# Attention over feature pairs on one core: sixteen identity matmuls first, one transposition later, three loads on another queue

## The chip, the core and the metric

The kernel runs on one core of a Trainium2 chip. Its engines are TensorE (PE, with its weight loads PEld), VectorE (DVE), ScalarE (ACT), GpSimd (POOL) and SyncE (SP), each with its own list of instructions, tied together by semaphores. The metric is device time in microseconds; the number given is a median of runs.

## The reference

512 samples have 33 embedding rows of 128 numbers each, gathered from tables. All 528 pairs of rows are multiplied element by element, go through a 128 x 128 layer with relu, and are scored against the sample's GNN feature. A softmax over the pairs weighs the products, and a three-layer MLP follows. All is fp32.

```python
inner = x[:, row] * x[:, col]                       # 528 pairs
fm = relu(einsum('bpd,ad->bpa', inner, attn_W) + attn_b)
attn = softmax(einsum('ba,bpa->bp', gnn_feature, fm), axis=1)
attn_output = einsum('bp,bpd->bd', attn, inner) * 100.0
h = concatenate([gnn_feature, attn_output, gnn_feature], axis=1)
h = maximum(h @ W_top1 + b_top1, 0.0)
h = maximum(h @ W_top2 + b_top2, 0.0)
y = h @ W_top3
```

## The kernel before

The batch is cut into 4 tiles of 128 samples, and a tile into 32 steps of 4 samples. One step is: VectorE multiplies the pairs of four samples (`product`, L757) into one of two slots of `inner`; TensorE runs six rounds of 352 columns through the attention weights (`pair_products`, L466) into four banks of `x_ps`; ScalarE applies the relu to each round (L700) into `fm`; TensorE takes the scores (`scores`, L478), with a column of GNN features that VectorE has placed (`column`, L773). TensorE's order is: products of step s, then scores of step s - 1. VectorE's `column` of a step waits for the scores two steps back, and the next `product` stands behind it.

The rows come in groups of 128 (4 samples x 32 fields), one group for a step. GpSimd gathers a group with one indirect DMA (L364). For the first tile it issues twelve groups at once (`FIRST_RUN`), then three more after each step's scores (`scores_done`). Four groups are a chunk. Gathered rows have to be turned: TensorE transposes them into `m_ps` (L485 for whole groups, L523 for half rows, two chunks at a time), and VectorE copies them into `e_t` (`copy_chunk`, `copy_half`). Which chunk is turned after which step of the first tile stands in `FIRST_TURNS`, and the copies in `FIRST_COPIES`. The opening is apart: `turn_opening` turns the last field's rows and group 0, `turn_opening_rest` groups 1 to 3, so that the first product can begin early.

Before the steps, TensorE computes the GNN part of the first MLP layer (`gnn_layer(c)`, L587, four chunks of two calls), once `gnn_t` and two parts of `w1` have landed. ScalarE reads each result out (L726). Then it issues three DMAs from its own queue: the third part of `w1`, `w2` and `w3` (L728 to L730), needed in the MLP at the end of the kernel. SyncE starts with four loads, and then waits for `zeros_cleared`, which GpSimd gives in the first tile at step `AHEAD_AT` = 24. The identity `ident` is made by GpSimd at the start (L356, L358).

Of the kernel before, what the change touches and what calls it, by code (L numbers as in the profile page):

```python
# [36 lines left out]
P = 128  # L37
# [54 lines left out]
NEXT_AT = 8  # L92
AHEAD_AT = 24
FOLD_AT = POOL_AT - 2
FIRST_TURNS = {3: (2, 3), 6: (4, 5), 9: (6, 7)}
FIRST_COPIES = {2: 1, 5: 2, 6: 3, 8: 4, 9: 5, 11: 6, 12: 7}
OPENING = 2
LAST_FIELDS_AT = 18
HALF_ROWS = P // 2
# [2 lines left out]
H1, H2 = 512, 256  # L102
# [3 lines left out]
def flat(tensor_ap, offset, dims):  # L106

    return bass.AP(tensor=tensor_ap.tensor, offset=offset, ap=dims)


def build(nc, gnn_cols, gnn_pairs, ids, table, w_top1, b_top1, w_top2, b_top2, w_top3, attn_w_cols, attn_b, out):
    band_dram = nc.dram_tensor("band_scratch", (P, BAND), F32, kind="Internal").ap()

    with ExitStack() as ctx:
# [18 lines left out]
        ident = sb("ident", [P, P])  # L133
# [11 lines left out]
        w1 = sb("w1", [P, K1, H1])  # L145
        w2 = sb("w2", [P, C1, H2])
        w3 = sb("w3", [P, C2])
# [10 lines left out]
        x_ps = ctx.enter_context(nc.psum_tensor("x_ps", [P, 4, BANKF], F32))  # L158
# [11 lines left out]
        w1_attn_loaded = sem("w1_attn_loaded")  # L170
        w23_loaded = sem("w23_loaded")
        ident_zero = sem("ident_zero")
        ident_ready = sem("ident_ready")
# [128 lines left out]
        @block.sync  # L302
        def _(sp):
            sp.dma_start(idx_in[:, :], ids).then_inc(ids_loaded, 16)
            sp.dma_start(gnn_t[:, :], gnn_cols).then_inc(gnn_t_loaded, 16)
            sp.dma_start(attn_w_t[:, :], attn_w_cols).then_inc(attn_w_loaded, 16)
            sp.dma_start(gnn_z[:, :, :], gnn_pairs).then_inc(gnn_z_loaded, 16)

            def store_bands(stage, m0, m1):
                issue_bands(sp, stage, m0, m1)  # L310
                sp.wait_ge(band_stored, bands_per_stage * (stage + 1))

            def load_band(slot, free_at, row, groups=GPB):

                if free_at is not None:
                    sp.wait_ge(pool_done, free_at)
                for r in range(GROUP):
                    sp.dma_start(band[r * SIDE:(r + 1) * SIDE, slot, 0:groups, r, :],
                                 flat(band_dram, row * BAND + r * BAND,
                                      [[WIDE, SIDE], [GROUP * BAND, groups], [1, WIDE]])  # L320
                                 ).then_inc(pool_loaded[slot], 16)

            def load_bands(t):
                for k in range(2):
                    load_band(k, POOL_N * t if t else None, ROWS * k)
                with sp.Fori(1, POOLS // 2) as i:
                    for slot in range(2):
                        load_band(slot, 2 * i + (POOL_N * t + slot - 1), 2 * ROWS * i + ROWS * slot)
                load_band(0, POOL_N * t + POOLS - 1, POOLS * ROWS, LEFT_GROUPS)
                for slot in range(2):  # L330
                    sp.wait_ge(pool_loaded[slot], pool_per_tile[slot] * (t + 1))

            sp.wait_ge(zeros_cleared, 1)
            sp.dma_start(band_dram, zeros[:, :]).then_inc(bands_zeroed, 16)
            sp.wait_ge(bands_zeroed, 16)
            sp.wait_ge(bands_cleared, 2)
            for t in range(LAST):
                store_bands(t, 0, STEPS)
                load_bands(t)

            store_bands(LAST, STAGE_M[0], STAGE_M[1])
            for k in range(L_BATCHES):
                load_band(k % 2, POOL_N * LAST + max(k - 1, 0), ROWS * k)
            issue_bands(sp, LAST + 1, STAGE_M[1], STAGE_M[2])
            issue_tail_bands(sp, 1)

            issue_bands(sp, LAST + 2, STAGE_M[2], STAGE_M[3], turned_around=(0, 1))
            issue_tail_bands(sp, 2)
            sp.wait_ge(y_ready, len(MLP_PARTS))
            sp.dma_start(out.rearrange("b o -> o b"), y[:, :]).then_inc(y_stored, 16)  # L350
            sp.wait_ge(y_stored, 16)
# [103 lines left out]
        def _(pe):  # L455
# [31 lines left out]
            def turn_opening():  # L487

                pe.wait_ge(ident_ready, 1)
                pe.wait_ge(last_gathered[0], 16)  # L490
                pe.transpose(m_ps[:, 1, 0:P], last_rows[:, 0, :], ident[:, :])
                pe.wait_ge(first_gathered, 16)
                turn_group(0, 0, 0).then_inc(turned, 1)
# [16 lines left out]
            def turn_chunks(t, chunks):  # L510

                pe.wait_ge(turn_copied, turns_through(t, chunks[0]) - 1)
                for c in chunks:
                    pe.wait_ge(gathered[t % BUFFERS][c], 16 * CHUNK * (t // BUFFERS + 1)
                               - (16 if t == BUFFERS and c == 0 else 0))
                    for g in range(CHUNK * c, CHUNK * c + CHUNK):
                        if len(chunks) == 1:
                            mm = turn_group(c % 2, t, g)
                        else:
                            at = (g - CHUNK * chunks[0]) * HALF_ROWS  # L520
                            for h in range(2):
                                lo, hi = HALF_ROWS * h, HALF_ROWS * (h + 1)
                                mm = pe.transpose(m_ps[:, h, at:at + HALF_ROWS], rows[lo:hi, t % BUFFERS, g, :],  # L523
                                                  ident[lo:hi, lo:hi])
                mm.then_inc(turned, len(chunks))
# [59 lines left out]
            def gnn_layer(c):  # L585
                for k in (0, 2):
                    mm = pe.matmul(x_ps[:, c, :], w1[:, k, c * P:(c + 1) * P], gnn_t[:, :],  # L587
                                   start=(k == 0), stop=(k == 2))
                mm.then_inc(gnn_layer_done, 1)


            pe.wait_ge(gnn_t_loaded, 16)
            pe.wait_ge(w1_loaded, 32)
            gnn_layer(0)
            turn_opening()
            gnn_layer(1)
            gnn_layer(2)
            turn_opening_rest()
            gnn_layer(3)
# [2 lines left out]
            for t in range(TILES):  # L602
                base = STEPS * t

                pair_products(base, 0, first=t == 0)
                if t == 0:
                    turn_chunks(0, (1,))
                else:
                    scores(base - 1, 1, stop=True)
                pair_products(base + 1, 1)  # L610
                if t > 0:
                    pe.wait_ge(exp_done, t)
                scores(base, 0, start=True)
                for s in range(2, POOL_AT + POOLS if t > 0 else POOL_AT + 2):
                    pair_products(base + s, s % 2)
                    scores(base + s - 1, (s - 1) % 2)
                    if t == 0 and s in FIRST_TURNS:
                        turn_chunks(0, FIRST_TURNS[s])
                    if t > 0 and s >= POOL_AT:
                        pool_step(t - 1, s - POOL_AT)  # L620
                if t == 0:
                    with pe.Fori(1, POOLS // 2) as i:
                        for j in range(2):
                            pair_products(2 * i + (base + POOL_AT + j), j)
                            scores(2 * i + (base + POOL_AT + j - 1), 1 - j)
                if t == LAST:
                    break

                for s in range(POOL_AT + POOLS, STEPS):
                    pair_products(base + s, s % 2)  # L630
                    scores(base + s - 1, (s - 1) % 2)
                    if t > 0 and s == POOL_AT + POOLS:
                        pool_step(t - 1, POOLS)
                    if t == 0 and s == LAST_FIELDS_AT:
                        turn_last_fields()
                    if s == TURN_AT and t > 0:
                        pe.wait_ge(pool_read, POOL_N * t)
                    if s in TURNS:
                        turn_chunks(t + 1, TURNS[s])
# [16 lines left out]
            for g in range(TAIL_GROUPS):  # L656
                k = g // GPB
# [25 lines left out]
        def _(act):  # L683
            def w1_part(k):
                return flat(w_top1, k * P * H1, [[H1, P], [1, H1]])
# [38 lines left out]
            for c in range(C1):  # L724
                act.wait_ge(gnn_layer_done, c + 1)
                act.activation(h1_gnn[:, c, :], x_ps[:, c, :], ACT.Identity,  # L726
                               bias=b1[:, c:c + 1]).then_inc(gnn_layer_read, 1)
            act.dma_start(w1[:, 1, :], w1_part(1)).then_inc(w1_attn_loaded, 16)  # L728
            act.dma_start(w2[:, :, :], w_top2.rearrange("(k p) n -> p k n", p=P)).then_inc(w23_loaded, 16)
            act.dma_start(w3[:, :], w_top3.rearrange("(k p) o -> p (k o)", p=P),  # L730
                          allow_slow_non_contiguous=True).then_inc(w23_loaded, 16)
            for t in range(TILES):
                base = STEPS * t
                relus(base, 0, first=t == 0)
# [262 lines left out]
```

## Time and profile before

| what | value |
|---|---|
| runs before | median 651.45 us (651.18 to 651.52, 3 runs) |
| profiled execution, its own time | 656.16 us |
| its span | 654.4 us |
| TensorE busy | 641.9 us (98%) |
| VectorE, ScalarE, GpSimd busy | 403.6, 417.4, 268.8 us |
| granted TensorE clock, mean | 0.999 |

The span goes from the first to the last instruction of the profile. Busy times of the engines lie beside one another, and a matmul's end is modelled, so TensorE's share is not a share of its peak. Times in rows below are microseconds from the start of the span unless they are marked ns.

### The profile page before, as it was taken

The page shows a single profiled execution, that of the slowest core. Times are in us where ns is not written, and L with a number is a line of the kernel's source. Part 1 is how long each engine was busy: PE and PEld are TensorE (multiplying, and loading weights), DVE is VectorE, ACT ScalarE, POOL GpSimd, SP SyncE. Part 2 cuts the span into 40 slices and gives each one's busy share as a digit, 9 for nine tenths or more (in the row PEclk, how much of TensorE's full clock was granted, in tenths as well). Part 3 has the DMA queues.
Part 4 walks back from the last instruction along what each step waited for, and adds up shares of the span by engine and source line. Part 5 has one row for each costly group of instructions (what it writes and reads, how often), then busy time and mean ns, then how long its engine had stood idle before and what let it go on. Part 6 is the DMA issues. An engine that isn't in the chain of part 4 may idle for free.

```text
span 654.4 us, 22667 instructions
## 1 busy us (share of the span) xinstructions
PE 641.9 (98%) x9596; PEld 328.1 (50%) x9596; DVE 403.6 (62%) x426; ACT 417.4 (64%) x797; POOL 268.8 (41%) x208
## 2 busy tenths in 40 slices
PE   6998999999999999999999999999999999999998
PEld 2444444444444555544444555544444555544566
DVE  3564655656664677676655577766655567764763
ACT  2665666666777566676777556667677666677651
POOL 6787876685656422244746522244101011100010
PEclk9999999999999999999999999999999999999999
DMA  3211111011091111000092111000026011030010
GB/s 117 83 37 37 30 36 30 25 30 64 18 31 27 28 32 26 16 13 18 14 32 30 24 32 30 16 18 6 1 14 15 7 17 18 7 21 8 16 25 8
DMA packets 51286, 17.29 MB, mean 26 GB/s; under 512 B 47553, under 2 KB 48321, under 8 KB 51202
## 3 DMA queue, kind: packets, MB, share of 16 engines
q1 hardware_dynamic: 44738, 6.03, 11.3%
q0 software_dynamic: 4288, 8.66, 5.5%
q8 instruction: 73, 1.20, 0.8%
q10 hardware_dynamic: 2176, 1.32, 0.7%
q14 instruction: 11, 0.09, 0.1%
HBM read 14.10 MB, written 1.89 MB: 24 GB/s over the span
## 4 chain that ended last, share of the span: by engine, by line
PE 91%; DVE 2%; POOL 2%; DMA 2%; another core or an unknown queue 1%; issue 1%; ACT 0%; DVEq 0%; ACTq 0%
PE x_ps L466 66%; PE s_ps L478 16%; PE m_ps L531 4%; POOL rows L364 2%; DVE inner L757 2%; PE m_ps L523 1%; DMA rows<-in_table,idx 1%; PE s_ps L571 1%; PE x_ps L571 1%; PE x_ps L531 1%; DMA idx_in<-in_ids 0%; PE x_ps L560 0%; DVE e_t L809 0%; PE m_ps L560 0%
## 5 line engine op out<-in xcount | busy, mean ns | idle before, releaser
L700 ACT ACTIVATE fm<-x_ps,ab 128x352 f32<-128x352 f32 x768 | 406.0, 555 | 204.3 <-PE x_ps L466 184.2
L466 PE MATMUL x_ps<-inner,attn_w_t 128*32 128x352 f32 x6144 | 480.8, 459 | 2.2 <-issue 0.9
L466 PEld LDWEIGHTS x_ps<-inner,attn_w_t 128*32 128x32 f32 x6144 | 201.5, 110 | 229.7 <-issue 149.4
L757 DVE TENSOR_TENSOR inner<-e_t 128x2112 f32<-128x2112 f32 (+1 forms) x128 | 302.0, 2359 | 19.3 <-PE x_ps L466 16.6
L364 POOL DMA_INDIRECT rows<-in_table,idx x128 | 213.0, 1664 | 196.5 <-PE s_ps L478 179.9
L478 PE MATMUL s_ps<-fm,gnn_col 128*32 128x256 f32 (+1 forms) x2048 | 138.0, 386 | 0.0
L773 DVE COPY gnn_col<-gnn_z 128x8 f32<-128x8 f32 (+1 forms) x120 | 23.9, 199 | 180.0 <-PE s_ps L478 173.0
L478 PEld LDWEIGHTS s_ps<-fm,gnn_col 128*32 128x32 f32 x2048 | 68.7, 110 | 62.4 <-issue 20.5
L392 POOL TENSOR_TENSOR band<-band 128x192 f32<-128x192 f32 (+1 forms) x39 | 26.3, 676 | 145.6 <-DMA band<-band_scratch 145.1
L531 PE MATMUL m_ps<-band,rows 128*32 128x132 f32 x912 | 33.5, 275 | 0.0
L531 PEld LDWEIGHTS m_ps<-band,rows 128*32 128x32 f32 x912 | 27.9, 109 | 7.1
L826 DVE TENSOR_REDUCE attn_out<-pooled 128x396 f32 (+2 forms) x44 | 24.4, 553 | 4.8
L809 DVE COPY e_t<-m_ps 128x512 f32<-128x512 f32 x30 | 19.6, 686 | 8.1 <-PE m_ps L523 6.2
L822 DVE TENSOR_TENSOR pooled<-m_ps,e_t 128x396 f32<-128x396 f32 (+1 forms) x40 | 22.2, 555 | 0.7
L382 POOL COPY e_t<-e_t 128x256 f32<-128x256 f32 x24 | 13.3, 583 | 9.3 <-DVE e_t L809 9.2
L587 PE MATMUL x_ps<-gnn_t,w 128*128 128x512 f32 x16 | 10.3, 790 | 5.4 <-DMA w<-in_W_top 5.4
L523 PEld LDWEIGHTS m_ps<-ident,rows 64*128 64x128 f32 x240 | 8.8, 138 | 7.7 <-issue 6.6
L523 PE MATMUL m_ps<-ident,rows 64*128 64x64 f32 x240 | 11.1, 229 | 0.8 <-DMA rows<-in_table,idx 0.8
L370 POOL DMA_INDIRECT last_rows<-in_table,idx x4 | 7.5, 1871 | 3.8 <-DVE idx L868 2.9
L587 PEld LDWEIGHTS x_ps<-gnn_t,w 128*128 128x128 f32 x16 | 3.8, 260 | 8.9 <-DMA gnn_t<-in_gnn_cols 5.4
L779 DVE COPY gnn_col<-gnn_z 128x4 f32<-128x4 f32 x6 | 1.0, 172 | 11.7 <-PE s_ps L478 11.7
L392 POOL TENSOR_TENSOR tail_band<-tail_band 128x640 f32<-128x640 f32 (+1 forms) x2 | 2.0, 996 | 15.0 <-DMA tail_band<-band_scratch 15.0
(57 smaller groups left out, 86.5 us busy)
## 6 DMA issues: line engine op xcount, KB each, us to landing
band<-band_scratch SPq DMA_DIRECT2D x144, 18.4 KB
rows<-in_table,idx POOLq DMA_INDIRECT x128, 2.5
band_scratch<-zeros SPq DMA_DIRECT2D x1, 784.0 KB, 3.3
w<-in_W_top ACTq DMA_DIRECT2D x3, 256.0 KB
band_scratch<-attn SPq DMA_DIRECT2D x12, 64.0 KB
gnn_z<-in_gnn_pairs SPq DMA_DIRECT2D x1, 512.0 KB
w<-in_W_top ACTq DMA_DIRECT2D x1, 512.0 KB
gnn_t<-in_gnn_cols SPq DMA_DIRECT2D x1, 256.0 KB, 3.8
```

Source lines behind the costliest of these rows:

```text
L364: pool.indirect_dma_start(rows[:, t % BUFFERS, g, :], None, table, bass.IndirectOffsetOnAxis(ap=idx[:, STEPS * t + g:STEPS * t + g + 1], a ...
L392: pool.tensor_tensor(view[:, :, 0:HOPS], view[:, :, 0:HOPS], view[:, :, FIELDS:WIDE], ALU.add).then_inc(done, 1)
L466: mm = pe.matmul(strip(x_ps[:, (ROUNDS * slot + r) % 4, 0:ROUND], c), strip_of(attn_w_t, c), round_of(inner, slot, r), start=True, stop=True)
L478: mm = pe.matmul(s_ps[32 * q:32 * q + 32, h, score_at[h]:score_at[h] + hi - lo], gnn_col[:, slot, q, :], fm[:, slot, q, lo:hi], start=star ...
L523: mm = pe.transpose(m_ps[:, h, at:at + HALF_ROWS], rows[lo:hi, t % BUFFERS, g, :], ident[lo:hi, lo:hi])
L531: mm = pe.matmul(strip(out, c).rearrange("p (r w) -> p r w", w=FIELDS), strip_of(fields, c), bands[:, :, 0:FIELDS], start=True, stop=True)
L700: act.activation(round_of(fm, slot, r), x_ps[:, (ROUNDS * slot + r) % 4, 0:ROUND], ACT.Relu, bias=ab[:, 0:1]).then_inc(fm_ready, 1)
L757: dve.tensor_tensor(inner[:, slot, :, :].rearrange("p q (i k) -> p q i k", k=HOPS), flat(e, at, [[P * WIDE, P], [WIDE, QUADS], [1, FIELDS] ...
L773: dve.tensor_copy(col_at(slot, m - 2, 2), gnn_at(t, m, 0, 2)).then_inc(col_ready, 1)
L809: done = dve.tensor_copy(flat(e_t[t % 2][:, :, :], at, dims + [[1, SIDE]]), src)
L822: dve.tensor_tensor(sums, bank[:, 0:n_rows * FIELDS].rearrange("p (r w) -> p r w", w=FIELDS), flat(e_t[t % 2][:, :, :], row * WIDE, [[P * ...
L826: dve.tensor_reduce(flat(attn_out[:, :], t * P + row, [[BATCH, P], [1, n_rows]]), sums, AX.X, ALU.add).then_inc(pool_summed, 1)
```

## The change

Sixteen fp32 matmuls of the identity with itself stand ahead of TensorE's wait for `gnn_t`; they write 128 columns of `x_ps`, which `gnn_layer(0)` overwrites. The opening turn moves from behind `gnn_layer(0)` to behind `gnn_layer(1)`. The turn of chunk 1 moves from behind the products of step 0 to behind the products of step 1 and the scores of step 0, and its copy from behind step 2 to behind step 3. The three MLP loads leave ScalarE's queue for SyncE's, where they wait for the twelfth `scores_done`.

```diff
-FIRST_TURNS = {3: (2, 3), 6: (4, 5), 9: (6, 7)}
-FIRST_COPIES = {2: 1, 5: 2, 6: 3, 8: 4, 9: 5, 11: 6, 12: 7}
+FIRST_TURNS = {1: (1,), 3: (2, 3), 6: (4, 5), 9: (6, 7)}
+FIRST_COPIES = {3: 1, 5: 2, 6: 3, 8: 4, 9: 5, 11: 6, 12: 7}
+WARM_UPS = 16
+WEIGHTS_AT = 12
...
+            sp.wait_ge(scores_done, WEIGHTS_AT)
+            sp.dma_start(w1[:, 1, :], flat(w_top1, P * H1, [[H1, P], [1, H1]])).then_inc(w1_attn_loaded, 16)
+            sp.dma_start(w2[:, :, :], w_top2.rearrange("(k p) n -> p k n", p=P)).then_inc(w23_loaded, 16)
+            sp.dma_start(w3[:, :], w_top3.rearrange("(k p) o -> p (k o)", p=P),
+                         allow_slow_non_contiguous=True).then_inc(w23_loaded, 16)
             sp.wait_ge(zeros_cleared, 1)
...
+            pe.wait_ge(ident_ready, 1)
+            for _ in range(WARM_UPS):
+                pe.matmul(x_ps[:, 0, 0:P], ident[:, :], ident[:, :], start=True, stop=True)
             pe.wait_ge(gnn_t_loaded, 16)
             pe.wait_ge(w1_loaded, 32)
             gnn_layer(0)
+            gnn_layer(1)
             turn_opening()
-            gnn_layer(1)
             gnn_layer(2)
...
                 pair_products(base, 0, first=t == 0)
-                if t == 0:
-                    turn_chunks(0, (1,))
-                else:
+                if t > 0:
                     scores(base - 1, 1, stop=True)
                 pair_products(base + 1, 1)
                 if t > 0:
                     pe.wait_ge(exp_done, t)
                 scores(base, 0, start=True)
+                if t == 0:
+                    turn_chunks(0, FIRST_TURNS[1])
...
-            act.dma_start(w1[:, 1, :], w1_part(1)).then_inc(w1_attn_loaded, 16)
-            act.dma_start(w2[:, :, :], w_top2.rearrange("(k p) n -> p k n", p=P)).then_inc(w23_loaded, 16)
-            act.dma_start(w3[:, :], w_top3.rearrange("(k p) o -> p (k o)", p=P),
-                          allow_slow_non_contiguous=True).then_inc(w23_loaded, 16)
```

## Rows read from the trace of the kernel before

**Rows 1.** The page, part 4: the chain that ended last, by engine

```profile
PE 91%; DVE 2%; POOL 2%; DMA 2%; another core or an unknown queue 1%; issue 1%; ACT 0%; DVEq 0%; ACTq 0%
```

**Rows 2.** The chain in order of time, 0 to 60 us: start, length, what

```profile
16.34 4.46 DMA rows<-in_table,idx
...
32.27 3.59 DMA rows<-in_table,idx
...
52.90 6.87 another core or an unknown queue
```

**Rows 3.** Timeline, TensorE and its loads: start, length, engine, line, tiles, count, [idle before]

```profile
5.40 3.75 PE L587 MATMUL x_ps<-gnn_t,w 128*128 128x512 f32 x4 [5.40 <-DMA w<-in_W_top]
...
9.16 0.42 PE L485 MATMUL m_ps<-ident,rows 128*128 128x128 f32 x1
...
11.08 0.34 PEld L587 LDWEIGHTS x_ps<-gnn_t,w 128*128 128x128 f32 x1 [0.52 <-issue]
11.72 0.19 PEld L587 LDWEIGHTS x_ps<-gnn_t,w 128*128 128x128 f32 x1 [0.30 <-issue]
12.15 0.19 PEld L587 LDWEIGHTS x_ps<-gnn_t,w 128*128 128x128 f32 x1 [0.24 <-issue]
...
16.00 3.76 PE L466 MATMUL x_ps<-inner,attn_w_t 128*32 128x352 f32 x48
...
21.26 0.63 PE L485 MATMUL m_ps<-ident,rows 128*128 128x128 f32 x4 [1.50 <-DMA rows<-in_table,idx]
```

**Rows 4.** Busy time by stretch: PE, PEld, DVE, ACT, POOL, granted clock, DMA, GB/s

```profile
10.00:15.00 5.00, 5.00 (x13) 2.28 (x12) 3.21 (x5) 2.58 (x4) 4.17 (x3) 1.00 0.15 39
```

**Rows 5.** Timeline, GpSimd's gathers

```profile
10.88 2.65 POOL L364 DMA_INDIRECT rows<-in_table,idx  x1 [0.30 <-issue]
...
31.02 0.95 POOL L364 DMA_INDIRECT rows<-in_table,idx  x1 [0.30 <-issue]
32.27 2.03 POOL L364 DMA_INDIRECT rows<-in_table,idx  x1 [0.30 <-issue]
```

**Rows 6.** Timeline, VectorE: products (L757), column copies (L773), copies of turned rows

```profile
9.62 0.38 DVE L873 COPY e_t<-m_ps 128x128 f32<-128x128 f32 x1 [5.29 <-issue]
...
10.35 2.36 DVE L757 TENSOR_TENSOR inner<-e_t 128x2112 f32<-128x2112 f32 x1
...
14.39 0.56 DVE L786 COPY e_t<-m_ps 128x384 f32<-128x384 f32 x1 [1.68 <-PE m_ps L485]
...
15.32 2.36 DVE L757 TENSOR_TENSOR inner<-e_t 128x2112 f32<-128x2112 f32 x1
...
26.54 0.17 DVE L773 COPY gnn_col<-gnn_z 128x8 f32<-128x8 f32 x1 [3.99 <-PE s_ps L478]
...
27.55 2.35 DVE L757 TENSOR_TENSOR inner<-e_t 128x2112 f32<-128x2112 f32 x1
...
30.98 0.25 DVE L773 COPY gnn_col<-gnn_z 128x8 f32<-128x8 f32 x1 [1.08 <-PE s_ps L478]
...
31.14 2.35 DVE L757 TENSOR_TENSOR inner<-e_t 128x2112 f32<-128x2112 f32 x1
```

**Rows 7.** Timeline: third step's products, their first relu and scores; later steps

```profile
26.29 3.73 PE L466 MATMUL x_ps<-inner,attn_w_t 128*32 128x352 f32 x48
...
27.13 0.55 ACT L700 ACTIVATE fm<-x_ps,ab 128x352 f32<-128x352 f32 x1 [0.93 <-PE x_ps L466]
...
29.84 1.07 PE L478 MATMUL s_ps<-fm,gnn_col 128*32 128x256 f32 x16
...
36.30 4.02 PE L466 MATMUL x_ps<-inner,attn_w_t 128*32 128x352 f32 x48
...
51.90 3.76 PE L466 MATMUL x_ps<-inner,attn_w_t 128*32 128x352 f32 x48
```

**Rows 8.** Timeline, ScalarE's queue: the last of its three loads

```profile
16.97 0.53 ACTq L730 DMA_DIRECT2D w<-in_W_top  x1
```

**Rows 9.** Waits of SyncE's queue: total, times, longest

```profile
SPq L334 <- POOL zeros L425: 144.0, 1, 144.0
```

## The prediction

> **What bounds the kernel now.** I read the page first. The chain that ended last is TensorE for nine tenths [rows 1], so a change pays only where TensorE stands still. Then the chain in order of time, for where it leaves TensorE: nearly everything lies before 60 us. GpSimd's gathers stand in it twice, once up to the gather that lands at 20.80 (16.34 + 4.46) and once up to the one that lands at 35.86; then comes a piece of 6.87 that the profile can't name [rows 2]. After that it is steps of 4.44 (VectorE's column copies of two steps, 26.54 and 30.98 [rows 6]), which the diff leaves alone. So the question is when the rows of the first tile are gathered, turned and multiplied.
>
> The timeline, engine by engine, gives the mechanism. In the opening TensorE's 512-column matmuls are slow: loads at 11.08 and 11.72, then every 0.43 (11.72, 12.15), and the first four take 3.75 [rows 3]. That is about 0.86 each against 0.43: half rate and full rate, as between the chip's levels of 1.2 and 2.4 GHz, though the granted clock column says 1.00 (2.4) in this stretch too [rows 4]. TensorE had worked from 5.40 to about 11.4, 6.0 us, before it was fast.
>
> GpSimd writes a gather in 0.95 and starts the next 0.30 later, so 1.25 each. But a gather that starts while VectorE multiplies (2.36 for one step) is held until that product ends, and 0.81 more: 32.27 to 34.30, with a product that ends at 33.49 (31.14 + 2.35). One that starts 0.12 before the product is not held (31.02) [rows 5, 6]. All nine held ones up to 54 us end 0.81 to 0.83 behind their product. The data lands 1.56 after the end (34.30 to 35.86 [rows 2, 5]).
>
> **The change, part by part.** I follow group numbers g0 to g15 (g7 completes chunk 1, g15 chunk 3) and products P0, P1, ... of the steps.
>
> Warm-ups: sixteen fp32 calls are 32 instructions (a call makes two here, as the four instructions at 5.40 are gnn_layer(0)'s two calls). At 128 columns I take a quarter of 0.86, so 0.21, slow and 0.11 fast. No row shows identity matmuls back to back; bounds are 32 x 0.11 = 3.4 (all fast) and 32 x 0.34 = 10.9 (each waiting for its load of 0.34 [rows 3]). I take 0.21 for the first 6.0 us and 0.11 after, since matmuls and loads overlap in these rows. They start at about 1.55, when the identity is made: 28 slow to 7.5, 4 fast to 7.95. The layer could start at 5.40 before, so this is 2.5 late.
>
> Layer and opening: gnn_layer(0) and (1), 8 x 0.43, end at 11.4. The opening turn is now behind both, at 11.5 (before, 9.16). VectorE's first copy followed it by 0.46 and P0 by 0.73 more (9.62, 10.35 [rows 6]); fast, I take 0.35 and 0.73: P0 at 12.56, 2.2 later than before, ending at D = 14.92. TensorE: 11.37 + 0.22 + 1.71 (layer 2) + 0.33 + 1.71 (layer 3) + 0.09 gives the first step at 15.43, 0.57 earlier than 16.00 [rows 3]. ScalarE's three loads no longer sit before its first relu (the last issue runs 16.97 to 17.50 [rows 8]), so the first step runs the 3.55 of an undisturbed one (26.29 to 29.84 [rows 7]) and not 3.76 [rows 3].
>
> The turn of chunk 1: before, TensorE waited 1.50 for g7 (21.26 [rows 3]) with the second step ready. Now both steps run, the first column of scores is done, and the turn (0.63) comes at 15.43 + 2 x 3.55 + 0.89 = 23.42. The second step is therefore over at 22.5 instead of 21.89 + 3.55 = 25.4: some 3 us gained, if nothing else is late.
>
> What is late next is GpSimd. The third and later gathers still cost 1.25 each plus holds; what goes is only its idle time before g12, which waits for the first step's scores. A step's result reaches others 0.84 behind its start and 0.59 more per round, 3.79 in all (26.29, 27.13 [rows 7]); scores take 1.07 from 3.55 on (29.84), the column follows 0.07 later, and the next product 0.16 behind the column, or 1.01 if a chunk is copied between (26.54, 27.55; 30.98, 31.14 [rows 6]). P1 follows P0's end by 0.93 (14.39, 15.32), because the turn is ready. The walk:
>
> g4 10.88, g5 12.13 free. g6 13.38 is in P0: held to 15.74. g7 16.04 is in P1 (15.85 to 18.21): to 19.03. g8 19.33 is in P2 (from 19.28): to 22.46. g9 free. g10 24.01 is in P3 (from 23.83): to 27.01. g11, g12 free. g13 29.81 is in P4 (from 29.75): to 32.93. g14 33.23 starts 0.11 before P5 (33.34 to 35.70): free. g15 34.48 is in P5: to 36.52, landing 38.08. TensorE has stood at the turn of chunks 2 and 3 since 32.93.
>
> So the fifth step begins at 38.08 + 0.44 = 38.52, against 36.30 [rows 7]: 2.2 later. Some of it comes back: from 36.30 to 51.90 before took 15.60; three steps of 4.44 and a turn of 0.65 are 13.97, and the 1.63 between them are waits, for g23 and for late relus, that I take to fall away: after 36.52 the gathers g16 to g23 have 10.0 of pitch and about three holds ahead of them, and TensorE asks at 51.8. 38.52 + 13.97 = 52.49, 0.6 later than 51.90.
>
> SyncE's loads: SyncE waited 144.0 for the cleared zeros [rows 9], and nothing stands behind the new wait but that. The twelfth scores are at some 80 us, the weights are wanted behind the last step: 0. If the cover failed, three issues of 0.53 [rows 8] would delay a store by 1.6.
>
> Sum: 0 (loads) + 0.6 (everything before 52 us) on the profiled 656.16. That execution is 4.71 longer than the median, 651.45, and part of it may be the unnamed 6.87 [rows 2]; I carry the difference over unchanged: 652.1.
>
> A page speaks to the hold. Trace: 0.81 behind the product [rows 5, 6]. The Trainium skill, SBUF — State Buffer, A bandwidth-pool intuition that's wrong, has a GpSimd DMA blocked until the VectorE instruction's end and about 115 ns. By that figure g15 would end at 35.82 and not 36.52, and the sum would be an estimated 0.1 under the kernel before instead of 0.6 over. The trace doesn't agree on the size, and I go by its rows.
>
> **The rivals.** Three margins in the walk are 0.05 to 0.11 (g8 against P2, g13 against P4, g14 against P5), and each flip moves g15 to another slot.
>
> Faster: one flips in favour (g13 or g8 gets ahead of its product). Then g15 has g14's place, ends at 34.18, lands at 35.74, and the end is 2.34 earlier than forecast: 1.7 under before, 649.7. For it: TensorE is some 2.4 early at the turn of chunks 2 and 3 (32.93; before, 36.30 less two chunks of 0.5), and holds in the trace lose 1.1 to 2.2 each, while mine are mostly 2. Against it: two margins must not flip back. 0.28.
>
> Slower: g14 also falls in P5. g14 ends at 36.52, g15 runs 36.82 to 37.77 and lands at 39.33: 1.25 later than forecast, 653.3. It decides from g14 starting after P5. For it: the products now stand closer together, so every one catches a gather. 0.23.
>
> Dear warm-ups (0.34 each): they end at 12.4, the first step starts near 19.9, TensorE reaches the turn at 37.4 and the fifth step starts near 38.5, as forecast; up to 1 later where g15 is held again: 652.1 to 653.1. 0.05.
>
> No effect at all: the gathers give the whole gain at TensorE back and no more. That is g15 landing at 37.5, 0.6 earlier than in the walk, and lies inside the forecast's range.
>
> **How the numbers follow.** Forecast 0.44, its own range 650.8 to 652.7. What can be told from no change here is 0.2%, 1.3 us: 650.15 to 652.75. The forecast and part of the last rival lie inside: same 0.44; faster 0.28; slower 0.23 + 0.05 = 0.28. The range takes in the first two rivals' values, with 0.4 for the sizes taken: 649.3 to 653.7.
>
> **What would show it.** Full-rate loads by 8 us and the layer's first load near 8; first step near 15.4; product P0 near 12.6; the turn of chunk 1 with no wait, at 23.4; a wait of 2 to 5 us for a gather before the turn of chunks 2 and 3; gathers of 2 to 3 us in nearly every product. I'm wrong if g15 lands before 36, if warm-ups take over 8 us, or if the unnamed piece near 57 us changes size: then the difference isn't mine.

## The result, and the profile after

| what | before | after |
|---|---|---|
| median of runs | 651.28 us (650.3 to 651.8, 22 runs) | 654.37 us |
| ratio, after to before | | 1.0034, 95% interval 1.0021 to 1.0047 |
| profiled execution, its own time | 656.16 us | 653.97 us |
| its span, mean granted clock | 654.4 us, 0.999 | 652.2 us, 0.997 |

The change makes the kernel slower by about a third of a per cent. One run at 747 us, and one of the kernel before at 842 us beside experiments 9 and 10, were disturbed as a whole and are left out of the ratios and of what follows. The other 21 don't lie around their median but in two groups with nothing between them: 6 runs at 650.09 to 650.95 (median 650.8), all with a granted clock of 1.000, and 15 at 653.97 to 655.38 (median 654.7), with clocks of 0.993 to 0.997. That is why the two medians alone would give 1.0047, and the means of the same runs (653.5 and 651.2) 1.0034. The runs before lie in one band. The profiled execution after is the fastest run of the upper group.

The chain of this execution in order of time (start, length, what) has one long gather left, where before had two and an unnamed piece [rows 2]:

```profile
33.33 4.60 DMA rows<-in_table,idx
...
37.97 0.69 PE m_ps L530 x6
38.66 4.83 PE x_ps L473 x48
...
44.38 3.55 PE x_ps L473 x48
```

The timeline of the same execution, line by line against the walk of the prediction (all engines; length is that of a merged group):

```profile
1.53 6.35 PE L601 MATMUL x_ps<-ident 128*128 128x128 f32 x32 [1.53 <-POOL ident L365]
...
7.72 3.60 PE L594 MATMUL x_ps<-gnn_t,w 128*128 128x512 f32 x8
...
12.31 2.36 DVE L763 TENSOR_TENSOR inner<-e_t 128x2112 f32<-128x2112 f32 x1
12.53 2.95 POOL L371 DMA_INDIRECT rows<-in_table,idx  x1 [0.30 <-issue]
...
15.23 7.31 PE L473 MATMUL x_ps<-inner,attn_w_t 128*32 128x352 f32 x96
...
23.36 0.66 PE L492 MATMUL m_ps<-ident,rows 128*128 128x128 f32 x4
...
33.18 2.36 DVE L763 TENSOR_TENSOR inner<-e_t 128x2112 f32<-128x2112 f32 x1
33.33 3.03 POOL L371 DMA_INDIRECT rows<-in_table,idx  x1 [0.30 <-PE s_ps L485]
...
37.97 0.69 PE L530 MATMUL m_ps<-ident,rows 64*128 64x64 f32 x8 [4.55 <-DMA rows<-in_table,idx]
...
38.59 4.90 PE L473 MATMUL x_ps<-inner,attn_w_t 128*32 128x352 f32 x48
...
40.06 0.55 ACT L710 ACTIVATE fm<-x_ps,ab 128x352 f32<-128x352 f32 x1 [7.29 <-PE x_ps L473]
...
41.20 2.92 ACT L710 ACTIVATE fm<-x_ps,ab 128x352 f32<-128x352 f32 x5 [0.59 <-PE x_ps L473]
```

Identity matmuls end at 7.9 (1.53 + 6.35), the GNN layer starts at 7.72, P0 at 12.31, the first step at 15.23, two steps run together as one group of 96 matmuls, and the turn of chunk 1 comes at 23.36 with no wait, where before TensorE waited 1.50 [rows 3]. P5 starts at 33.18, g15 at 33.33, 0.15 inside it: it is held to 36.36, which is 0.82 behind the product, as in [rows 5, 6]. TensorE stands 4.55 for it (the bracket of the row at 37.97) and goes on at 37.97. The next step's 48 matmuls then take 4.90 instead of 3.76, and two relus start 1.14 apart instead of 0.59 (40.06, 41.20). Why, the busy time by stretch shows (columns: PE, PEld, DVE, ACT, POOL busy, granted clock, DMA, GB/s):

```profile
30.00:35.00 5.00, 3.42 (x56) 1.52 (x47) 4.11 (x3) 2.61 (x5) 4.39 (x3) 1.00 0.17 37
35.00:40.00 5.00, 2.03 (x20) 1.10 (x24) 0.54 (x1) 0.00 (x0) 4.08 (x4) 0.75 0.15 39
40.00:45.00 5.00, 5.00 (x68) 2.03 (x64) 0.54 (x2) 3.32 (x6) 2.29 (x4) 0.90 0.18 43
```

The granted clock is 0.75 in 35 to 40 us and 0.90 in 40 to 45. Half clock (1.2 GHz) for half of the first five us and a fifth of the second gives these values: 3.5 us. Read in stretches of half a microsecond, it fell at about 37.5, while TensorE still stood, and came back at about 41.0. The Trainium skill, TensorE: Matmul & The Clock Gate, HAM oscillation — how this bites in real kernels, says that a wait for data in which TensorE idles can throttle it again, so that the next work starts slow; the trace agrees, with 4.55 us of standing and a step that takes 1.18 longer (38.59 to 43.32, against 3.55).

### The profile page after: what moved, and what is told of

Read it like the earlier page. It is cut to its first block, busy times and chain, and to the rows that moved or that the text cites. A ratio compares the mean times of both kernels' runs of the same rounds, so it can differ in the third digit from the quotient of the medians.

```text
span 652.2 us, 22731 instructions
## 1 busy us (share of the span) xinstructions
PE 643.4 (99%) x9628; PEld 332.2 (51%) x9628; DVE 403.5 (62%) x426; ACT 434.5 (67%) x797; POOL 266.6 (41%) x208
## 4 chain that ended last, share of the span: by engine, by line
PE 96%; issue 2%; DVE 1%; DMA 1%; POOL 0%; ACT 0%; POOLq 0%; DVEq 0%
PE x_ps L473 70%; PE s_ps L485 17%; PE m_ps L538 4%; PE m_ps L530 1%; PE x_ps L594 1%; PE x_ps L601 1%; DMA rows<-in_table,idx 1%; DVE inner L763 0%; PE x_ps L578 0%; PE s_ps L578 0%; POOL band_scratch L279 0%; ACT h L725 0%; PE x_ps L567 0%; PE m_ps L492 0%; PE x_ps L587 0%
## 5 line engine op out<-in xcount | busy, mean ns | idle before, releaser
L710 ACT ACTIVATE fm<-x_ps,ab 128x352 f32<-128x352 f32 x768 | 423.2, 554 | 185.5 <-PE x_ps L473 163.6
L371 POOL DMA_INDIRECT rows<-in_table,idx x128 | 210.0, 1641 | 196.1 <-PE s_ps L485 180.7
L389 POOL COPY e_t<-e_t 128x256 f32<-128x256 f32 x24 | 14.7, 639 | 9.3 <-DVE e_t L815 9.2
L601 PE MATMUL x_ps<-ident 128*128 128x128 f32 x32 | 6.3, 389 | 1.5 <-POOL ident L365 1.5
```

The lines of the kernel that those rows point to most:

```text
L371: pool.indirect_dma_start(rows[:, t % BUFFERS, g, :], None, table, bass.IndirectOffsetOnAxis(ap=idx[:, STEPS * t + g:STEPS * t + g + 1], a ...
L710: act.activation(round_of(fm, slot, r), x_ps[:, (ROUNDS * slot + r) % 4, 0:ROUND], ACT.Relu, bias=ab[:, 0:1]).then_inc(fm_ready, 1)
```

## The experiments

Each ran beside the kernel before, on the same chip; "before" below is its median there.

**1. The kernel before, a second profile.** No edit.

> The kernel before, unchanged, for a second profile. Theory (the profile of before, 656.16, was taken of an execution with late semaphores, which the timed runs at 651.3 don't have): a span near 649.6, the second half of the turn of chunks 4 and 5 still held for g23 near 50 to 52 us, and steps of 4.44 with nothing unnamed. Rival (the unnamed piece of 6.87 belongs to the kernel): it stands there again near 55 us.

It took 650.94 (before 651.51). Timeline, TensorE:

```profile
14.64 3.76 PE L466 MATMUL x_ps<-inner,attn_w_t 128*32 128x352 f32 x48
20.20 0.63 PE L485 MATMUL m_ps<-ident,rows 128*128 128x128 f32 x4 [1.81 <-DMA rows<-in_table,idx]
...
34.84 0.46 PE L523 MATMUL m_ps<-ident,rows 64*128 64x64 f32 x8 [0.16 <-DMA rows<-in_table,idx]
35.23 3.76 PE L466 MATMUL x_ps<-inner,attn_w_t 128*32 128x352 f32 x48
...
50.32 0.46 PE L523 MATMUL m_ps<-ident,rows 64*128 64x64 f32 x8 [1.17 <-DMA rows<-in_table,idx]
```

No unnamed piece, and everything 1.1 to 1.4 earlier than in the profile on which I had worked: first step 14.64 for 16.00, fifth step 35.23 for 36.30. The expected wait for g23 is there, 1.17 at 50.32. So the profile of before had been taken of an execution 4.7 us longer than the runs, and this one is the better yardstick.

**2. The later turn of chunk 1 alone.**

```diff
-FIRST_TURNS = {3: (2, 3), 6: (4, 5), 9: (6, 7)}
-FIRST_COPIES = {2: 1, 5: 2, 6: 3, 8: 4, 9: 5, 11: 6, 12: 7}
+FIRST_TURNS = {1: (1,), 3: (2, 3), 6: (4, 5), 9: (6, 7)}
+FIRST_COPIES = {3: 1, 5: 2, 6: 3, 8: 4, 9: 5, 11: 6, 12: 7}
...
-                if t == 0:
-                    turn_chunks(0, (1,))
-                else:
+                if t > 0:
...
                 scores(base, 0, start=True)
+                if t == 0:
+                    turn_chunks(0, FIRST_TURNS[1])
```

> Of the change only the later turn of chunk 1. Theory (the cost sits in gathers that fall into products, and in which slot g15 gets): the opening is that of before, g4 falls into the first product, and g15 should start before the fifth product ends or ahead of it, landing at 33 to 35.5, when TensorE asks for it at about 33.8: no wait of over 2 us, and 649.5 to 651.0. Rival (the later turn by itself is what makes TensorE run into a long wait): a wait of 4 us or more before the turn of chunks 2 and 3, and 653 to 655.

It took 653.14 (before 651.51), ratio 1.0023 (1.0000 to 1.0047), in two groups: 7 runs at 649.96 to 653.39 at clock 0.999 or 1.000, 5 at 655.1 to 656.4 at 0.993 to 0.995. The profile has the early slot (g15 held by P4, wait 1.22). My number was a miss: neither does this part gain reliably nor is it free of the upper group. The rival is half right. Its five upper runs were not profiled. In the profiled run P0 starts at 10.37 and g5 only at 13.85, so what parts these two groups is open. That run is 2.45 over experiment 1, but only some 0.55 of it stands behind the first tile; 1.82 is a piece at 343.02 for which the chain names no cause.

**3. Identity matmuls and the later opening turn alone.**

```diff
+WARM_UPS = 16
...
+            pe.wait_ge(ident_ready, 1)
+            for _ in range(WARM_UPS):
+                pe.matmul(x_ps[:, 0, 0:P], ident[:, :], ident[:, :], start=True, stop=True)
...
             gnn_layer(0)
-            turn_opening()
             gnn_layer(1)
+            turn_opening()
```

> Of the change only the sixteen identity matmuls and the opening turn behind the second GNN chunk. Theory (gather slots): TensorE waits for g7 before the turn of chunk 1 as before; P0 near 12.3 holds g5 or g6, P1 near 15.5 the next, so g7 lands at about 20 to 20.5, and the time is 651 to 653. Rival (the late opening alone is the cost of the change): 654 to 655, in two groups as with the whole change.

It took 652.93 (before 651.51), ratio 1.0014 (1.0005 to 1.0023), within what the theory had. Timeline, TensorE:

```profile
15.67 3.76 PE L467 MATMUL x_ps<-inner,attn_w_t 128*32 128x352 f32 x48
22.01 0.63 PE L486 MATMUL m_ps<-ident,rows 128*128 128x128 f32 x4 [2.58 <-DMA rows<-in_table,idx]
```

The first step starts at 15.67, a full 1.0 later than in the undisturbed profile of before (14.64), and g7 is then waited for 2.58. So this part delays the first step and gains nothing. g7 was expected at 20 to 20.5 and lands at 21.87, as the chain shows:

```profile
16.23 5.64 DMA rows<-in_table,idx
```

GpSimd ends its part of this gather at 19.13 (16.23 + 2.90), so the data comes 2.74 behind it, where the prediction has 1.56. In the profile of before it comes 2.30 behind (18.50 to 20.80). In both, ScalarE's three loads come at that time (the last issue ends at 17.50 in [rows 8]): the DMA engines are busy for 0.65 and 0.63 of 15 to 20 us, and for 0.12 in the changed kernel, whose loads come later. That the loads delay g7 fits and was not run alone. Six of the twelve runs have a clock of 0.996; none of those was profiled.

**4. The changed kernel, a second profile.**

> The changed kernel again, for a second profile. Its timed runs lie in two groups, near 650.6 at a granted clock of 1.000 and near 654.5 at 0.995. Theory: the groups are the two slots of g15. In the upper one it falls into P5, TensorE stands over 4 us, and then runs at half clock for a while; in the lower one g15 has the slot before, TensorE stands under 2.5 us and keeps its clock. Which one comes out is set by g5 against P0. Rival: g15 lands at the same time in both groups and only the clock differs.

652.06 (before 651.51), clock 0.999. Timeline, all engines:

```profile
12.49 0.94 POOL L371 DMA_INDIRECT rows<-in_table,idx  x1 [0.30 <-issue]
...
12.64 2.36 DVE L763 TENSOR_TENSOR inner<-e_t 128x2112 f32<-128x2112 f32 x1
...
13.74 2.08 POOL L371 DMA_INDIRECT rows<-in_table,idx  x1 [0.30 <-issue]
...
19.32 0.94 POOL L371 DMA_INDIRECT rows<-in_table,idx  x1 [0.30 <-issue]
...
19.46 2.36 DVE L763 TENSOR_TENSOR inner<-e_t 128x2112 f32<-128x2112 f32 x1 [1.11 <-PE x_ps L473]
...
31.14 2.22 POOL L371 DMA_INDIRECT rows<-in_table,idx  x1 [0.30 <-issue]
...
34.98 0.47 PE L530 MATMUL m_ps<-ident,rows 64*128 64x64 f32 x8 [1.22 <-DMA rows<-in_table,idx]
...
35.38 1.08 PE L473 MATMUL x_ps<-inner,attn_w_t 128*32 128x352 f32 x10
```

Here g5 starts at 12.49 and P0 at 12.64: g5 is free, all later gathers are one group ahead, g15 starts at 31.14, is held by P4 and not P5, and TensorE waits 1.22 and not 4.55. What moved between the two profiles is P0 and not g5 (12.53 and 12.49): the identity matmuls took 6.35 there and 6.68 here. The fifth step starts at 35.38. The rival (same landing, other clock) is out: g15 ends at 33.36 here and at 36.36 in the upper group. Up to the turn of chunks 4 and 5 it is level with experiment 1 (its second half starts at 50.41, against 50.32), and so it is up to 480 us; the 1.1 between the two times comes behind that, in parts that the change doesn't touch.

**5 to 8. 14 and 18 identity matmuls, a filled wait, later turns; on a chip with late relus.**

```diff
-WARM_UPS = 16
+WARM_UPS = 14        # 18 in experiments 6 and 10
```

> The changed kernel with 14 identity matmuls, so that TensorE, and the first product with it, is some 0.4 us earlier (P0 near 11.9 to 12.2) while the gathers stay. Theory (g5 against P0 decides): g5 always starts inside P0, g15 has the late slot in every run, TensorE stands about 4.5 to 5 us at the turn of chunks 2 and 3 and the granted clock falls: nearly all runs in the upper group, 653.5 to 655.5, at 0.993 to 0.997. Rival (the two groups have another cause): both groups again in about the same shares, or two matmuls less make it a little faster.

> The changed kernel with 18 identity matmuls: P0 near 12.75 to 13.1, TensorE's work 0.4 us later. Theory: g5 always starts ahead of P0, g15 has the early slot, lands near 35 with a wait of under 2 us, and the upper group is gone: 650.3 to 652.2, clock 0.999 or 1.000. Rival (more identity matmuls are more delay): 0.4 slower than the changed kernel, both groups still there.

The filled wait, on top of 14 (the `wait_ge` lets the relus of the step read their results before the identity matmuls overwrite them):

```diff
+FILLERS = 18
...
+                    if t == 0 and s == 3:
+                        pe.wait_ge(fm_ready, ROUNDS * 4)
+                        for _ in range(FILLERS):
+                            pe.matmul(x_ps[:, 0, 0:P], ident[:, :], ident[:, :], start=True, stop=True)
                     if t == 0 and s in FIRST_TURNS:
```

> As the kernel with 14, and TensorE multiplies the identity 18 times more (36 instructions, 3.9 us) where it stands before the turn of chunks 2 and 3; the results are overwritten. Theory (the wait costs twice: g15's landing, and then half clock): g15 lands when it did, the granted clock stays at 1.0 in 35 to 45 us, and the time is 1.2 to 2.5 under that of the kernel with 14. Rival (the half clock costs nothing that the wait hasn't cost already): same time as with 14, or up to 0.5 more.

The later turns, on top of the changed kernel:

```diff
-FIRST_TURNS = {1: (1,), 3: (2, 3), 6: (4, 5), 9: (6, 7)}
-FIRST_COPIES = {3: 1, 5: 2, 6: 3, 8: 4, 9: 5, 11: 6, 12: 7}
+FIRST_TURNS = {1: (1,), 4: (2, 3), 7: (4, 5), 9: (6, 7)}
+FIRST_COPIES = {3: 1, 6: 2, 7: 3, 9: 4, 10: 5, 11: 6, 12: 7}
```

> The changed kernel with the turns of chunks 2 and 3 after step 4 and of 4 and 5 after step 7 (copies a step later too); 6 and 7 stay after step 9. Theory (TensorE asks for gathers too early, its own work is there to be done): it asks for g15 at 37.4, when it has landed or lands within 1 us in either group; no granted clock under 1.0; it then waits for g31 about 1 to 3 us near 62. The upper group is gone and the time 649 to 651. Rival (the gathers bound the first tile anyway, the wait only moves to g31): 650.5 to 654.5 as before, with a wait of 4 us near 62 and the clock falling there.

On this chip the kernel before itself took 655.87 (654.4 to 658.1). Medians and ratios: 14, 656.42, 1.0006 (0.9990 to 1.0021); 18, 655.39, 0.9985 (0.9969 to 1.0000); filled, 659.43, 1.0046 (1.0029 to 1.0063); later turns, 654.93, 0.9987 (0.9971 to 1.0002). Timeline of the kernel with 14, TensorE and ScalarE:

```profile
28.67 2.55 PE L473 MATMUL x_ps<-inner,attn_w_t 128*32 128x352 f32 x32
...
31.63 0.55 ACT L710 ACTIVATE fm<-x_ps,ab 128x352 f32<-128x352 f32 x1 [2.89 <-PE x_ps L473]
...
33.80 1.44 ACT L710 ACTIVATE fm<-x_ps,ab 128x352 f32<-128x352 f32 x3 [1.61 <-PE x_ps L473]
```

The step starts at 28.67 and its first relu at 31.63, 2.96 later instead of 0.84 (26.29 and 27.13 in [rows 7]). Delays like this stand in all four profiles, and in the one of before with which I began. They move products and gathers by as much as the theory turns on, so these four runs neither bear it out nor refute it; the slots came out otherwise (with 18, g15 is held by no product). The filled kernel was expected 1.2 to 2.5 under the one with 14 and is 3.0 over it. In its profile GpSimd is done with g15 at 31.99, so g15 had landed before TensorE came to its turn, there was no wait to fill, and the identity matmuls only delay what follows:

```profile
36.94 4.84 PE L631 MATMUL x_ps<-ident 128*128 128x128 f32 x36
```

The four kernels therefore ran again.

**9 and 10. 14 against 18, again.**

> 14 identity matmuls once more, since the chip of the runs before showed relus that start 2 us behind their matmuls in every kernel, the kernel before included. Theory (slot of g15, then the clock): with P0 at 11.3 to 12.3 g5 starts inside it, g15 has the late slot; most runs near 654 to 655 at 0.995 to 0.997; where P0 starts before g4 (11.25), another slot. Rival: the shares of the groups are those of 16.

> 18 identity matmuls once more, beside the one with 14. Theory: g5 ahead of P0, g6 inside, g15 in the early slot, TensorE waits under 2 us: 650.3 to 652.2 in nearly all runs, clock 0.999 to 1.000. Rival: as with 14, or 0.4 slower than the changed kernel's own groups.

Before was 651.68. With 14: 653.69, ratio 1.0027 (1.0012 to 1.0041), 2 runs under 652 (clock 1.000) and 10 at 653.1 to 655.6 (0.995 to 0.997). With 18: 651.71, ratio 1.0008 (0.9992 to 1.0025), 10 runs at 650.4 to 652.4 (0.999 or 1.000) and 2 at 654.9 and 656.0 (0.994, 0.995). The upper group holds 10 of 12 runs with 14, 15 of 21 with 16 (another chip), 2 of 12 with 18. The theory stands: more identity matmuls, work for nothing, make the long wait rarer, since they move P0 behind the start of g5. In the two profiles they take 5.49 and 7.19, so four more calls move P0 by 1.70 (11.46 to 13.16), about twice of what I had expected. In the whole time 18 against 16 is not clear of noise (1.0008 and 1.0034, with intervals that overlap from 1.0021 to 1.0025). The slots are read in one profile of each kernel; for the other runs they are inferred from time and clock. Timeline of 14 (TensorE), and its stretches:

```profile
37.66 0.69 PE L530 MATMUL m_ps<-ident,rows 64*128 64x64 f32 x8 [4.54 <-DMA rows<-in_table,idx]
38.28 6.32 PE L473 MATMUL x_ps<-inner,attn_w_t 128*32 128x352 f32 x48
44.43 1.06 PE L485 MATMUL s_ps<-fm,gnn_col 128*32 128x256 f32 x16
```

```profile
35.00:40.00 5.00, 2.34 (x20) 1.09 (x24) 0.24 (x1) 0.25 (x1) 3.89 (x4) 0.67 0.16 42
40.00:45.00 5.00, 5.00 (x52) 1.90 (x48) 0.00 (x0) 2.84 (x6) 1.89 (x2) 0.65 0.17 40
```

Timeline of 18, all engines: g5 1.1 ahead of P0, and a wait of 1.30.

```profile
12.04 0.95 POOL L371 DMA_INDIRECT rows<-in_table,idx  x1 [0.30 <-issue]
...
13.16 2.36 DVE L763 TENSOR_TENSOR inner<-e_t 128x2112 f32<-128x2112 f32 x1
...
35.58 0.46 PE L530 MATMUL m_ps<-ident,rows 64*128 64x64 f32 x8 [1.30 <-DMA rows<-in_table,idx]
```

With 14, in this execution, the clock is at 0.67 and 0.65 in two stretches, 6.8 us at half, and the step behind the wait takes 6.15 (38.28 to 44.43) instead of 3.55: 2.6 us lost after a wait of 4.54. In the changed kernel's profile a wait of the same length lost 1.2. The loss varies, the wait doesn't. In half microseconds, the low clock lasts from 36.7 to 43.5 here, 5.8 us into the new work, and from 37.5 to 41.0 there, 3.0 us into it.

**11. The filled wait, again.**

> The filled wait (14 identity matmuls in front, 18 more before the turn of chunks 2 and 3), on a chip where relus follow their matmuls at once. Against the kernel with 14, whose median was 2.0 over before with the clock at 0.995 to 0.997. Theory (the half clock is a cost of its own, 1.2 after a wait of 4.55 with 0.997, 2.5 with 0.995): g15 lands near 37.6 as ever, the clock stays at 1.0, and the median is 0.3 to 1.0 over before. Rival (the clock costs nothing that the wait hasn't): 2.0 over before, as with 14.

It took 652.58 (before 651.51), ratio 1.0017 (1.0008 to 1.0026), eleven runs within 652.08 and 653.67, nearly all at 0.999 or 1.000. Timeline, TensorE, and stretches:

```profile
32.65 4.29 PE L631 MATMUL x_ps<-ident 128*128 128x128 f32 x36
...
37.68 0.46 PE L531 MATMUL m_ps<-ident,rows 64*128 64x64 f32 x8 [0.35 <-DMA rows<-in_table,idx]
38.07 3.76 PE L474 MATMUL x_ps<-inner,attn_w_t 128*32 128x352 f32 x48
41.65 1.07 PE L486 MATMUL s_ps<-fm,gnn_col 128*32 128x256 f32 x16
```

```profile
35.00:40.00 5.00, 4.65 (x62) 3.33 (x64) 0.22 (x1) 1.02 (x2) 3.88 (x4) 1.00 0.16 43
40.00:45.00 5.00, 5.00 (x80) 2.31 (x73) 2.21 (x4) 3.85 (x8) 3.57 (x4) 1.00 0.20 52
```

g15 is waited for as in experiment 9 (to 37.68, there 37.66), the clock is 1.00 throughout, and the step takes 3.58. The scores behind it start at 41.65 instead of 44.43: with the same landing, the clock alone makes 2.8 us. Over before, the median is 1.07, a little more than the 0.3 to 1.0 expected, against 2.0 with 14 unfilled. The ratio falls by 0.1% (from 1.0027), 0.7 us, but the two intervals overlap, so the whole times alone don't show it. That they show less than the rows has two reasons on record: 2 of the 12 unfilled runs had no long wait at all, and the profiled one (655.63) is the slowest of them. The spread is gone.

**12. The later turns, again.**

> The later turns (2 and 3 after step 4, 4 and 5 after step 7) with 16 identity matmuls, on such a chip. Theory: TensorE asks for g15 near 37.4, so in the late slot it waits under 1 us and its clock stays; the turn of 6 and 7 ends near 63 instead of 65.0: no upper group, 649.0 to 650.5, 1 to 2 under before. Rival (g31 takes over the wait): 651 or more, with a wait of over 3 us near 62.

A miss: 656.58 (before 651.51), ratio 1.0087 (1.0073 to 1.0102), over six runs, at clocks of 0.993 to 0.997. The profiled run, at 652.41 the fastest of them, has the expected start (no wait for g15, which has the early slot here, or for g23), and then this. Timeline, TensorE, and stretches:

```profile
62.74 0.47 PE L530 MATMUL m_ps<-ident,rows 64*128 64x64 f32 x8 [1.29 <-DVE e_t L817]
64.12 0.46 PE L530 MATMUL m_ps<-ident,rows 64*128 64x64 f32 x8 [0.92 <-DMA rows<-in_table,idx]
64.52 5.45 PE L473 MATMUL x_ps<-inner,attn_w_t 128*32 128x352 f32 x48
69.78 1.07 PE L485 MATMUL s_ps<-fm,gnn_col 128*32 128x256 f32 x16
```

```profile
60.00:65.00 5.00, 2.79 (x48) 1.46 (x44) 3.87 (x5) 1.11 (x2) 4.39 (x3) 1.00 0.11 26
65.00:70.00 5.00, 5.00 (x52) 1.96 (x45) 0.00 (x0) 2.77 (x5) 3.78 (x5) 0.66 0.17 43
```

Two waits of 1.29 (for VectorE's copy of chunk 5) and 0.92 (g31) with one half turn of 0.47 between them, and the clock is 0.66 in the next five us; the step takes 5.26 (64.52 to 69.78). The waits that were spread over the opening have moved to one place, and there they cost the clock. The slower five runs were not profiled; that they stand there longer is likely and not shown.

## Why the prediction was right and where it was not

**The walk held on TensorE.** Identity matmuls to 7.95 (measured 7.9), P0 at 12.56 (12.31), first step at 15.43 (15.23), turn of chunk 1 at 23.42 (23.36), arrival at the turn of chunks 2 and 3 at 32.93 (32.96), g15 held by P5 and landing at 38.08 (37.93), fifth step at 38.52 (38.59). The last expected sign, a wait of 2 to 5 us, is 4.55. That the gain of the later turn is spent in the queue of gathers is right, and is shown by experiments 4, 9 and 10.

**On GpSimd it came to the same place by another way.** The walk had g5 free and g6, g7, g8, g10 and g13 held. In the trace of the upper group g5, g6, g8, g10 and g14 are held, and g7 and g13 are free. It is five each time, so g15 comes into P5 (at 33.33, not 34.48), and whatever starts inside P5 ends behind it. That the landing agrees to 0.15 is owed to the place of P5 and to the equal count, and not to the order of the holds: in part luck.

**The sum did not hold.** The forecast was 0.6 over before, 652.1, with a range to 653.7. The ratio, on the 651.45 of the prediction, gives 653.7, just at the end of that range. The upper group, which is the forecast case, is 3.4 over (654.7 against 651.3). The sum can be checked between two profiles, the one after and experiment 1: the step behind the turn of chunks 4 and 5 starts at 53.84 against 50.71, 3.13 later, and the two executions differ by 3.03 in all (653.97, 650.94). Its terms:

- The baseline. "38.52, against 36.30: 2.2 later" used a disturbed execution. Undisturbed, the fifth step of before starts at 35.23: 38.59 is 3.36 later.
- The waits that fall away, taken as 1.63. Experiment 1 has 15.48 from 35.23 to 50.71, so 1.51 over the 13.97 of the sum, and after the change 0.10 of it is left. This term held.
- The clock. "Three steps of 4.44 and a turn of 0.65 are 13.97" took full rate for granted behind a stand of 4.6 us. The step behind it took 1.18 longer in the profile after, and 2.6 in that of experiment 9. I had the wait in the walk and the half rate in [rows 3] and [rows 4], and didn't put them together.

3.36 - 1.51 + 0.10 + 1.18 = 3.13. Mis-sized are the baseline, by 1.1, and the clock, put at nothing and 1.2. Most runs of the upper group have a clock of 0.995, like that of experiment 9, and not the 0.997 of the profiled one; that this makes the rest up to the group's 3.4 is likely and not shown. That the clock's share is a cost of its own and not a shadow of the wait is shown by the rows of experiments 9 and 11. The prediction had named a change of the unnamed piece near 57 us as a sign that the difference isn't the change's; the piece is gone after the change, but in experiment 1 as well, so it belongs to the execution profiled first.

**The rivals.** The faster one came: it is the lower group, 6 of 21 runs. In the profile of experiment 4 g5 to g7 are as in the walk, and the flip is one of the three that I had named: g8 starts at 19.32, 0.14 ahead of P2 at 19.46. From there g15 has g14's place, and it lands before 36, the sign against the forecast case. What I had missed is a fourth margin, g5 against P0, which I had called free at 12.13 against 12.56; the ids landed some 0.4 later in both profiles after (g5 at 12.53 and 12.49), and where P0 starts at 12.31 g5 is held. That margin parts the two profiles. The rival's price was wrong by the same baseline: the fifth step starts at 35.38 (experiment 4), 0.15 later than undisturbed before, and the lower group is 0.5 faster than before, not 1.7. The slower one (g14 in P5 too) is in no profile. Dear warm-ups fell: 32 matmuls in 6.35 us.

**The parts.** Warm-ups and opening alone cost 0.14% (experiment 3), the turn alone 0.23% with an interval down to 0 (experiment 2). The loads on SyncE were never run alone. The prediction put them at 0, and in the trace of the changed kernel their three issues begin at 81.53 and nothing waits there:

```profile
81.53 0.33 SPq L336 DMA_DIRECT2D w<-in_W_top  x1
```

Their absence from 15 to 20 us may let g7 land earlier (experiment 3); with the later turn of chunk 1 nothing waits for g7 even with the loads in place (experiment 2), so it would be worth nothing there.

No version beats the kernel before beyond its interval. The nearest to it is 18 identity matmuls: 1.0008 (0.9992 to 1.0025), and 0.9985 (0.9969 to 1.0000) on the chip with late relus.

**Left open:** what makes relus start 2 us behind their matmuls on one chip and in the first profile; why the clock came back after 3.0 us of work in one run and after 5.8 in another, with the same wait of 4.5 us ahead; what parts the two groups of experiment 2; and what the five slower runs of experiment 12 did.

## What to carry to other kernels

Where one queue (here GpSimd's gathers) is held by another engine's instruction, the time of a change is decided by which instruction starts first, at margins of 0.1 to 0.3 us: look for two groups in the runs, and shift one side by some dummy work (here four matmuls, 1.70 us between two profiles) to see them change places. Moving a wait was no gain here: several short ones of 1 to 2 us became one of 4.5, and the long one cost a second time in TensorE's clock. Before a change is priced against a profile, compare that execution's own time with the runs: 4.7 us of difference was more than everything at stake.

## What the runs showed of the hardware that was not expected

- A stand of 4.54 and 4.55 us of TensorE was followed by 6.8 and 3.5 us at half clock. Two shorter ones, 1.29 and 0.92 us with 0.47 of work between, were followed by 1.7 us lost at the same rate (0.66 of 65 to 70 us, so 3.4 us at half), while single stands of 1.22, 1.30 and 2.58 (experiments 4, 10 and 3) were followed by none.
- 36 identity matmuls of 128 columns took 4.29 us at full clock, 0.12 each, and kept the clock at 1.00 through a wait.
- A gather that GpSimd started while VectorE multiplied ended 0.82 behind the product (33.33 to 36.36, product to 35.54); one that started 0.15 ahead of the product was not held (12.49, product at 12.64).
- On one chip of those used, relus of some steps started 2.1 us later behind their matmuls than on the others (2.96 for 0.84), and the kernel before was 4.4 us longer (655.87 against 651.51). The changed kernels were not all longer there: with the later turns it was 1.7 shorter, filled 6.9 longer.
